# The second distance tile of each pair, made in the slot of the pair's first tile

## The chip, the cores and the metric

The kernel runs on one core of a Trainium2 chip. The metric is the device time of one execution in microseconds; lower is better. The engines have separate instruction queues and meet through semaphores: TensorE (PE in the profile, PEld for its weight loads), VectorE (DVE), ScalarE (ACT), GpSimd (POOL) and SyncE (SP), which here issues the DMAs.

## The reference

Two layers follow each other. The first is a chunked attention over `ctx` (32 batches, 128 channels, 1024 points; 8 heads, chunks of 64 points), with a residual and a normalisation along the points. The second works on the 30 nearest neighbours of each point, found by the distances between the columns of `ctx` of the same batch:

```python
def _knn(p, k):
    xx = jnp.sum(p * p, axis=1)
    pd = 2.0 * jnp.einsum('bdn,bdm->bnm', p, p) - xx[:, :, None] - xx[:, None, :]
    return jax.lax.top_k(pd, k)[1]
...
idx = _knn(x_loc, k)                       # x_loc is ctx, k is 30
pts = x_loc.transpose(0, 2, 1)
rel = pts[bidx, idx] - pts[:, :, None, :]  # first three channels are used
# rho, theta, phi of rel -> three small layers with batch norm -> softmax over the 30
agg = jnp.einsum('bnkc,bnk->bnc', xk, att)
return x + agg.transpose(0, 2, 1)
```

## The kernel before, in words

The kernel has three stages. `stage_a` does the attention, the distances, the search for the 30 nearest, and the gathering of their first three channels for all 32 batches; `stage_b` does the batch norms, `stage_e` the softmax and the weighted sum. Only `stage_a` is touched.

In `stage_a` the 1024 points of a batch are 8 tiles of 128 rows (`TILES`). Distances of tile t are a 128 x 1024 array, made as two halves of 512 columns (`distances(b, par, t, h)`; "D0" and "D1" in the prediction). Each half is two accumulated matmuls of TensorE (L407 and L409) into the one PSUM bank `pd_ps`, and a copy by ScalarE (its `distances`, through `move`, L588) into `pd_sb`, a ring of 4 tiles (`RING`). TensorE waits with a half until the copy before it is done (`pd_moved`), ScalarE waits with the first half of a tile until the tile that had its place has been sorted (`topk_done`).

VectorE works on tiles in pairs (0, 1), (2, 3), (4, 5), (6, 7). Four times (`RANKS`) it takes the 8 largest of each tile (MAX8, L866), finds their places (FIND_INDEX8, L871) and, the first three times, strikes them out (MATCH_REPLACE8, L873). The tiles of a pair alternate, so the second is wanted one MAX8 after the first. Between these it does the small steps of the attention: `largest(s)` (L896, the negated maximum of the scores, `mx`) behind the first and the third round, for the pair's first and second tile, each with `inverse` (L900, the reciprocal of the sums of exponentials of the tile before) ahead of it; `digits`, `row_stats` and `denoms` at fixed places. `gate` is a wait with a count.

TensorE and ScalarE go through the same slots t = 0 to 7, one for each tile, in an order written out by hand; h is the half of the batch and `quarter` the place in the half. A slot t has, in TensorE's order: turn_bits (quarter 0); unit; D0 of tile t + 2; unit; D1 of tile t + 2; unit; scores(t + 1); unit; turn_probs(t - 1); unit; values(t - 1); unit; the slot's extras; unit; unit. ScalarE has the copies that belong to them, and `exponents` (eight exponentials with their sums, L754) of tile t behind D0. The extras are: rows and project_values in slots 0 and 4, queries_keys in slots 2 and 6, squares in slot 3, norms in slot 5, and on ScalarE alone angles and rel_squares in slot 2 and roots in slot 4. Misc results use two PSUM banks in turn (`Misc`, `Moves`, `misc_ready`, `misc_moved`).

A unit is one rank of the 30 of the batch before: TensorE makes a one-hot matrix (`fill`, L482), ScalarE copies it (`one_hot`, `ohT`), TensorE multiplies it with the parts of the table (L503). TensorE is two fills ahead, ScalarE two copies. `unit_starts` gives 7, 8, 7 and 8 units to the slots of a half batch; each slot has eight calls of `unit()`, the last of which does nothing where there are 7.

scores(t + 1) wait for exponents(t) (`exp_ready`, one bank `s_ps`), `largest` waits for scores, exponents wait for `largest`. GpSimd normalises the exponentials (L1092, `normalise`) for turn_probs, spreads the keys (`spread_keys`, L1116, behind ScalarE's copy of `kt` in slots 2 and 6), multiplies and adds up what the units gathered, converts the digits (`convert`, L1126), and does the spherical coordinates of earlier batches (`sph_signs` and others), in an order of its own per slot.

A loop of the hardware runs over pairs of batches (`batches`: batches 0 to 3 and the last two are written out, the rest is `Fori`). In batch 0 there are no units.

Of the kernel before, what the change touches and what calls it, by code (L numbers as in the profile page):

```python
# [28 lines left out]
K = 30  # L29
EPS = 1e-5  # L30
TINY = 1e-20
TILES = T // P
QUADS = 2
QT = TILES // QUADS
# [111 lines left out]
def stage_a(nc, x, ctx, mask, w_in, b_in, w_out, b_out, consts, y_dram, cst, con, planes, idx_all, stats_all):  # L146
    OHR = 3
    XR = 97
    with ExitStack() as st:
# [121 lines left out]
        UNITS = QUADS * K  # L271
        NG = QUADS * GROUPS

        unit_starts = (0, 7, 15, 22, 30)
        slot_groups = [(4, 5), (0,), (1, 2), (3,)]

        FILLS = 31
# [26 lines left out]
        def there(d):  # L304

            return not isinstance(d, int) or d >= 0
# [54 lines left out]
        def _(pe):  # L361
# [37 lines left out]
            def distances(b, par, t, h):  # L399

                n = (b * TILES + t) * 2 + h

                if not (isinstance(n, int) and n < 1):
                    pe.wait_ge(pd_moved, n)
                if t == 0 and h == 0:
                    pe.wait_ge(xp_ready, b + 1)
                nc.tensor.matmul(pd_ps[:], ctx_s[:, par, bass.ts(t, P)], ctx_s[:, par, bass.ts(h, HALF)],  # L407
                                 start=True, stop=False)
                nc.tensor.matmul(pd_ps[:], ones3[0:XR, :], xp[0:XR, par, bass.ts(h, HALF)],  # L409
                                 start=False, stop=True).then_inc(pd_ready, 1)  # L410
# [74 lines left out]
            def gather(b, par, q, lo, hi, turned):  # L485

                if lo == 0:
                    pe.wait_ge(misc_moved, turned)
                    pe.wait_ge(split_step, (b + 1) * SPLITS)
                    fill(b, q, 0)  # L490
                    fill(b, q, 1)
                for k in range(lo, hi):
                    gu = b * UNITS + q * K + k
                    gi = q * GROUPS + k // GK
                    gg = b * NG + gi
                    if k + 2 < K:
                        fill(b, q, k + 2)
                    if k % GK == 0 and not (isinstance(gg, int) and gg < 2):
                        pe.wait_ge(g_moved, gg - 1)
                    pe.wait_ge(oh_moved, gu + 1)  # L500
                    for t in range(QT):
                        for part in range(PARTS):
                            m = nc.tensor.matmul(found_ps[gi % 2][:, k % GK, t, :], ohT[:, k % OHR, bass.ts(t, P)], tparts[:, par, part, :],  # L503
                                                 start=(part == 0), stop=(part == PARTS - 1))
                    if k % GK == GK - 1:
                        m.then_inc(g_ready, 1)

            def emit(b, j, par, first, last):
                misc = Misc(misc_base(b), first_bank(b, par))
                turned = None  # L510
                for t in range(TILES):
                    h, quarter = divmod(t, QT)
                    at = unit_starts[quarter]
                    end = unit_starts[quarter + 1]

                    def unit():
                        nonlocal at
                        if not first and at < end:
                            gather(b - 1, 1 - par, h, at, at + 1, turned)
                        at += 1  # L520

                    def ahead(half):

                        if t + 2 < TILES:
                            distances(b, par, t + 2, half)
                        elif not last:
                            distances(b + 1, 1 - par, t + 2 - TILES, half)

                    before = t > 0 or not first
                    nb, npar, nh = (b, par, 1) if h == 0 else (b + 1, 1 - par, 0)  # L530
                    ongoing = h == 0 or not last

                    if quarter == 0 and not first:
                        turned = turn_bits(misc, b - 1, h)
                    unit()
                    ahead(0)
                    unit()
                    ahead(1)
                    unit()
                    if quarter < QT - 1:  # L540
                        scores(b, par, t + 1)
                    elif ongoing:
                        scores(nb, npar, (t + 1) % TILES)
                    unit()
                    if before:
                        probs_in = turn_probs(misc, b if t > 0 else b - 1, (t - 1) % TILES)
                    unit()
                    if before:
                        moved = values(misc, (t - 1) % TILES, probs_in)
                    unit()  # L550
                    if quarter == 0 and before:
                        rows(misc, moved)
                    if quarter == 0:
                        project_values(misc, par, h)
                    if quarter == 2 and ongoing:
                        queries_keys(misc, npar, nh)
                    if t == 3 and not last:
                        squares(misc, b + 1)
                    if t == 5 and not last:
                        norms(misc, b + 1, 1 - par)  # L560
                    unit()
                    unit()

            def rows(misc, moved):

# [20 lines left out]
        def _(act):  # L586
# [38 lines left out]
            def distances(b, par, t, h, normed=None):  # L625
                s = b * TILES + t
                if t == 0 and h == 0:
                    act.wait_ge(misc_moved, normed)

                if h == 0 and not (isinstance(s, int) and s < RING):  # L630
                    act.wait_ge(topk_done, s - RING + 1)
                act.wait_ge(pd_ready, s * 2 + h + 1)
                move(pd_sb[:, t % RING, bass.ts(h, HALF)], pd_ps[:], scale=2.0,
                     bias=nxx[:, par, t:t + 1]).then_inc(pd_moved, 1)
# [36 lines left out]
            def emit(b, j, par, first, last):  # L671
                mv_ = Moves(misc_base(b), first_bank(b, par))
                normed = None
                for t in range(TILES):
                    h, quarter = divmod(t, QT)
                    at = unit_starts[quarter]
                    end = unit_starts[quarter + 1]

                    def unit():
                        nonlocal at  # L680
                        if not first and at < end:
                            gather(b - 1, h, at, at + 1)
                        at += 1

                    def ahead(half):
                        if t + 2 < TILES:
                            distances(b, par, t + 2, half)
                        elif not last:
                            distances(b + 1, 1 - par, t + 2 - TILES, half, normed)

                    before = t > 0 or not first
                    nb, nh = (b, 1) if h == 0 else (b + 1, 0)
                    ongoing = h == 0 or not last

                    if quarter == 0 and not first:
                        bits(mv_)
                    unit()
                    ahead(0)
                    exponents(b * TILES + t, t)
                    unit()  # L700
                    ahead(1)
                    unit()
                    unit()
                    if before:
                        turned_probs(mv_)
                    unit()
                    if before:
                        values(mv_, (t - 1) % TILES)
                    unit()
                    if quarter == 0 and before:  # L710
                        rows(mv_, b if t > 0 else b - 1, 0 if t > 0 else 1)
                    if quarter == 0:
                        project_values(mv_)
                    if quarter == 2 and ongoing:
                        queries_keys(mv_, nb, nh)
                    if t == 2:
                        if there(b - 3):
                            angles(b - 3)
                        if there(b - 2):
                            rel_squares(b - 2)  # L720
                    if t == 4 and there(b - 2):
                        roots(b - 2)
                    if t == 3 and not last:
                        squares(mv_, b + 1, 1 - par)
                    if t == 5 and not last:
                        normed = norms(mv_, 1 - par)
                    unit()
                    unit()

            def rel_squares(d):  # L730

# [44 lines left out]
            normed = norms(mv0, 0)  # L776
# [1244 lines left out]
```

## Time and profile before

| what | value |
|---|---|
| runs before | 5790.62 us median of 3 (5788.26 to 5792.64) |
| profiled execution, its own time | 5790.79 us |
| its span | 5788.7 us |
| mean granted clock of TensorE | 0.874 |
| busy: VectorE | 5127.8 us, 89% of the span |
| busy: TensorE | 4476.3 us, 77% |
| busy: ScalarE | 4035.6 us, 70% |
| busy: GpSimd | 3045.6 us, 53% |

The span is from the first to the last instruction; the execution's own time has 2.1 us more around it. `stage_a` ends at about 4025 us. Busy shares are over all three stages.

### The profile page before, as it was taken

The numbers are of one execution on the slowest core, as the hardware profiler recorded it, in microseconds if no ns is written. First come the engines' busy times: TensorE is split into PE (matmuls) and PEld (weight loads), VectorE is DVE, ScalarE is ACT, GpSimd is POOL, SyncE is SP. The second block draws the span as 40 slices with busy tenths as digits, with TensorE's granted clock in tenths as the row PEclk, the third lists the DMA queues.
The fourth block names the chain that finished last, engine by engine and source line by source line (L and its number), as shares of the span: only waits on it lengthen the run. The fifth ranks groups of instructions, "written<-read, shape, count | busy, mean of one in ns | idle before, by whom it ended". The sixth has DMA issues, their size and how long they took to land. (4 is left out here: it accounts for less than half of the span.)

```text
span 5788.7 us, 168877 instructions
## 1 busy us (share of the span) xinstructions
PE 4476.3 (77%) x62610; PEld 2718.6 (47%) x63182; DVE 5127.8 (89%) x7549; ACT 4035.6 (70%) x9505; POOL 3045.6 (53%) x3780
## 2 busy tenths in 40 slices
PE   5777777777777777777777777776395889999999
PEld 2444444444444444444444444443242666666666
DVE  7999989999989999998999998997398988888887
ACT  3777777777777777777777777776533766676666
POOL 3577777777777777777777777776400000000000
PEclk7888888888888898888888888887697899999999
DMA  0010000010000001000001000000000000000000
GB/s 29 16 31 16 16 17 16 17 31 16 17 16 17 17 16 32 16 17 16 17 17 31 17 16 17 16 16 12 1 0 8 25 30 27 30 26 30 26 30 26
DMA packets 135798, 114.60 MB, mean 20 GB/s; under 512 B 105344, under 2 KB 106112, under 8 KB 134784
## 3 DMA queue, kind: packets, MB, share of 16 engines
q1 hardware_dynamic: 134912, 102.73, 6.1%
q8 instruction: 563, 9.22, 0.7%
q14 instruction: 323, 2.65, 0.2%
HBM read 69.16 MB, written 33.55 MB: 18 GB/s over the span
## 5 line engine op out<-in xcount | busy, mean ns | idle before, releaser
L866 DVE MAX8 vals<-pd_sb 128x8 f32<-128x1024 f32 x1024 | 1200.6, 1211 | 302.2 <-ACT pd_sb L588 284.0
L588 ACT ACTIVATE ohT<-oh_ps 128x512 bf16<-128x512 f32 x1920 | 1152.0, 615 | 155.3 <-PE oh_ps L482 114.4
L871 DVE FIND_INDEX8 idx<-vals,pd_sb 128x8 uint16<-128x1024 f32 x1024 | 1244.6, 1218 | 0.0
L503 PEld LDWEIGHTS g_ps<-tparts,ohT 128*128 128x128 bf16 x23040 | 871.8, 99 | 380.9 <-issue 148.7
L503 PE MATMUL g_ps<-tparts,ohT 128*128 128x24 bf16 x23040 | 883.9, 175 | 81.6 <-issue 33.5
L873 DVE MATCH_REPLACE8 pd_sb<-vals,pd_sb 128x1024 f32<-128x1024 f32 x768 | 928.3, 1209 | 0.0
L1957 PEld LDWEIGHTS e_a_ps<-planes,e_oh 120*128 120x128 bf16 x24576 | 687.9, 97 | 299.5 <-issue 218.4
L482 PE MATMUL oh_ps<-bitsT,code 128*128 128x512 bf16 x1348 | 590.3, 442 | 293.4 <-ACT bitsT L772 155.7
L1727 ACT COPY e_at<-e_a_ps 128x512 f32<-128x512 f32 x512 | 543.1, 1061 | 356.1 <-PE e_a_ps L1957 349.8
L1957 PE MATMUL e_a_ps<-planes,e_oh 120*128 120x32 bf16 x24576 | 702.4, 178 | 83.2 <-DVE e_oh L1885 46.9
L754 ACT ACTIVATE sS<-s_ps,mx 128x64 f32<-128x64 f32 x2048 | 611.5, 329 | 169.4 <-DVE mx L896 168.1
L407 PE MATMUL pd_ps<-ctx_s 128*128 128x512 f32 x1024 | 656.3, 727 | 84.1 <-ACT pd_sb L588 82.9
L1885 DVE TENSOR_TENSOR e_oh<-e_pairs,e_iotan 120x2048 bf16<-120x2048 bf16 x512 | 623.9, 1219 | 3.4 <-PE e_a_ps L1957 1.1
L961 POOL TENSOR_TENSOR gsb<-gsb 128x240 f32<-128x240 f32 (+2 forms) x1152 | 544.5, 473 | 90.3
L482 PEld LDWEIGHTS oh_ps<-bitsT,code 128*128 128x128 bf16 x1920 | 192.8, 103 | 849.2 <-ACT ohT L588 360.8
L1116 POOL TENSOR_TENSOR kz<-kt,cst 128x1024 f32<-128x1024 f32 x256 | 484.3, 1902 | 172.2 <-ACT kt L588 101.0
L1971 PE MATMUL e_o_ps<-e_at,e_xT 128*128 128x512 f32 x1024 | 568.5, 650 | 0.2 <-ACT e_at L1727 0.2
L588 ACT ACTIVATE pd_sb<-pd_ps,nxx 128x512 f32<-128x512 f32 x512 | 366.2, 715 | 190.8 <-PE pd_ps L409 190.3
L1092 POOL TENSOR_TENSOR sS<-sS,rs 128x512 f32<-128x512 f32 x256 | 272.4, 1064 | 429.4 <-DVE rs L900 429.2
L754 ACT ACTIVATION_READ_ACCUMULATOR sS<-s_ps,mx 128x1 f32 x2048 | 455.1, 222 | 0.0
L958 POOL TENSOR_TENSOR gsb<-gsb,hi1h 128x480 f32<-128x480 f32 x384 | 439.9, 1146 | 12.5 <-DVE hi1h L835 8.7
L440 PE MATMUL s_ps<-xp,negs 32*64 32x512 bf16 x512 | 110.2, 427 | 370.2 <-ACT sS L754 367.0
(241 smaller groups left out, 7411.3 us busy)
## 6 DMA issues: line engine op xcount, KB each, us to landing
ctx_s<-in_ctx SPq DMA_DIRECT2D x32, 512.0 KB, 4.2
maskb<-in_mask_Bx1x_ff SPq DMA_DIRECT2D x32, 512.0 KB, 6.7
x_s<-in_x SPq DMA_DIRECT2D x32, 512.0 KB, 5.8
y_spill<-y_s SPq DMA_DIRECT2D x32, 512.0 KB, 3.0
e_y<-y_spill SPq DMA_DIRECT2D x32, 512.0 KB, 3.9
out<-e_o SPq DMA_DIRECT2D x64, 256.0 KB, 2.2
table<-in_ctx SPq DMA_DIRECT2D x96, 4.0 KB, 5.8
pd_sb<-in_shape_constants SPq DMA_DIRECT2D x1, 1180.0 KB, 5.4
```

Source lines behind the costliest of these rows:

```text
L407: nc.tensor.matmul(pd_ps[:], ctx_s[:, par, bass.ts(t, P)], ctx_s[:, par, bass.ts(h, HALF)], start=True, stop=False)
L482: nc.tensor.matmul(oh_ps[k % 2][:], code[:, k % KT, :], bitsT[:, k // KT, :], start=True, stop=True).then_inc(oh_ready, 1)
L503: m = nc.tensor.matmul(found_ps[gi % 2][:, k % GK, t, :], ohT[:, k % OHR, bass.ts(t, P)], tparts[:, par, part, :], start=(part == 0), stop ...
L588: return nc.scalar.activation(dst, src, func, scale=scale, bias=bias)
L754: m = nc.scalar.activation(sS[:, t % 2, hd, :], s_ps[:, hd, :], ACT.Exp, bias=mx[:, t % 2, hd:hd + 1], accum_out=rs[:, t % 2, hd:hd + 1])
L866: nc.vector.max(vals[:, i, :], pd_sb[:, (t + i) % RING, :]).then_inc(topk_step, 1)
L871: found = nc.vector.max_index(idx16[:, par, t + i, 8 * r:8 * r + 8], vals[:, i, :], work)
L873: nc.vector.match_replace(work, vals[:, i, :], work, REMOVED).then_inc(topk_step, 1)
L961: steps(nc.gpsimd.tensor_tensor(sums[:, :, 0:width], sums[:, :, 0:width], sums[:, :, width:2 * width], ALU.add))
L1885: v.tensor_tensor(oh[pp, g % RING], low.to_broadcast([QCOLS, NB // 2, LO, 2]), row.to_broadcast([QCOLS, NB // 2, LO, 2]), ALU.is_equal).th ...
L1957: m = nc.tensor.matmul(a_ps[g % 2][:, i].rearrange("p t e -> p (t e)"), oh[pp, g % RING, i // 2, :, i % 2], spr[q][pp, part, :, (g * NB + ...
L1971: m = nc.tensor.matmul(o_ps[q][:], xT[:, par, e, :], at[:, q, e].rearrange("p t n -> p (t n)"), start=(e == 0), stop=(e == HI - 1))
```

## The change

The distances of both tiles of the next pair are made in the even slot. Tile t + 2 stays where it was, in slot t with t even. Tile t + 3, which was made in slot t + 1 behind its first and its second unit, is made in slot t, behind `values` and one unit and ahead of the slot's extras. Odd slots make no distances. The calls of `unit()` become `units(place)` with a table of how many units stand at each of 8 places; between D0 and D1 of tile t + 3 (place 6) there is none, and the last place has one or two. The sums per slot are 7, 8, 7 and 8 as before. TensorE and ScalarE are changed alike.

```diff
-        unit_starts = (0, 7, 15, 22, 30)
+        units_at = ((1, 1, 1, 1, 1, 1, 0, 1),
+                    (1, 1, 1, 1, 1, 1, 0, 2),
+                    (1, 1, 1, 1, 1, 1, 0, 1),
+                    (1, 1, 1, 1, 1, 1, 0, 2))
+        unit_starts = [sum(sum(row) for row in units_at[:n]) for n in range(QT + 1)]
...
-                    def unit():
+                    def units(place):
                         nonlocal at
-                        if not first and at < end:
-                            gather(b - 1, 1 - par, h, at, at + 1, turned)
-                        at += 1
+                        n = units_at[quarter][place]
+                        if not first and n > 0:
+                            gather(b - 1, 1 - par, h, at, at + n, turned)
+                        at += n
...
-                    def ahead(half):
+                    def ahead(tiles, half):
-                        if t + 2 < TILES:
-                            distances(b, par, t + 2, half)
+                        if t + tiles < TILES:
+                            distances(b, par, t + tiles, half)
                         elif not last:
-                            distances(b + 1, 1 - par, t + 2 - TILES, half)
+                            distances(b + 1, 1 - par, t + tiles - TILES, half)
...
-                    unit()
-                    ahead(0)
-                    unit()
-                    ahead(1)
-                    unit()
+                    units(0)
+                    if t % 2 == 0:
+                        ahead(2, 0)
+                    units(1)
+                    if t % 2 == 0:
+                        ahead(2, 1)
+                    units(2)
...
-                    unit()
+                    units(5)
+                    if t % 2 == 0:
+                        ahead(3, 0)
+                    units(6)
+                    if t % 2 == 0:
+                        ahead(3, 1)
...
-                    unit()
-                    unit()
+                    units(7)
```

ScalarE's side has the same edit, with `exponents` where it stood, between `ahead(2, 0)` and `units(1)`.

## Rows read from the trace of the kernel before

**Rows 1.** The page's head: span and instructions.
```profile
span 5788.7 us, 168877 instructions
```

**Rows 2.** Waits from 365 to 4025 us: engine, line waited for, total, times, longest.
```profile
DVE vals L866 <- ACT pd_sb L588: 250.3, 31, 9.5
...
ACT sS L754 <- DVE mx L896: 139.7, 77, 5.2
```

**Rows 3.** Timeline of VectorE: start, duration, instruction, idle before it and releaser.
```profile
358.51 1.23 DVE L866 MAX8 vals<-pd_sb 128x8 f32<-128x1024 f32 x1 [5.51 <-ACT pd_sb L588]
...
2113.72 1.23 DVE L866 MAX8 vals<-pd_sb 128x8 f32<-128x1024 f32 x1 [8.36 <-ACT pd_sb L588]
...
2119.74 0.64 DVE L896 TENSOR_REDUCE mx<-s_ps 128x8 f32<-128x512 f32 x1
...
3994.10 1.23 DVE L866 MAX8 vals<-pd_sb 128x8 f32<-128x1024 f32 x1 [8.28 <-ACT pd_sb L588]
```

**Rows 4.** Timeline of TensorE, slots 4 and 5, and slot 4 a batch later.
```profile
2097.11 0.45 PE L503 MATMUL g_ps<-tparts,ohT 128*128 128x24 bf16 x12
2099.30 2.08 PE L568 MATMUL mi_ps<-oT,wT 128*128 128x512 f32 x2 [1.74 <-ACT oT L588]
...
2112.56 0.63 PE L440 MATMUL s_ps<-xp,negs 32*64 32x512 bf16 x2 [0.98 <-ACT sS L754]
2113.12 1.98 PE L444 MATMUL s_ps<-kz,qs 128*64 128x512 f32 x4
...
2219.84 1.09 PE L453 MATMUL mi_ps<-cst,sS 128*128 128x128 f32 x4 [2.58 <-POOL sS L1092]
...
2223.91 2.08 PE L568 MATMUL mi_ps<-oT,wT 128*128 128x512 f32 x2 [0.79 <-ACT oT L588]
```

**Rows 5.** Timeline of ScalarE, slots 4 and 5.
```profile
2101.50 0.69 ACT L588 ACTIVATE y_s<-mi_ps,bias 128x512 f32<-128x512 f32 x1 [1.76 <-PE mi_ps L568]
...
2108.02 0.69 ACT L588 ACTIVATE pd_sb<-pd_ps,nxx 128x512 f32<-128x512 f32 x1
...
2110.03 0.31 ACT L754 ACTIVATE sS<-s_ps,mx 128x64 f32<-128x64 f32 x1
...
2112.83 0.74 ACT L588 ACTIVATE pd_sb<-pd_ps,nxx 128x512 f32<-128x512 f32 x1
```

**Rows 6.** Timeline of TensorE: ends of slots 0, 2, 6, slot 4's start, slot 7.
```profile
2037.11 1.12 PE L568 MATMUL mi_ps<-oT,wT 128*128 128x512 f32 x2 [0.17 <-ACT oT L588]
...
2062.48 1.96 PE L416 MATMUL mi_ps<-ctx_s,wT 128*128 128x512 f32 x4
...
2086.26 2.05 PE L407 MATMUL pd_ps<-ctx_s 128*128 128x512 f32 x2
...
2130.66 1.12 PE L416 MATMUL mi_ps<-ctx_s,wT 128*128 128x512 f32 x2 [0.52 <-ACT oT L588]
...
2132.66 1.10 PE L407 MATMUL pd_ps<-ctx_s 128*128 128x512 f32 x2
2133.60 0.38 PE L409 MATMUL pd_ps<-xp,ones 97*128 97x512 bf16 x1
...
2134.76 1.13 PE L407 MATMUL pd_ps<-ctx_s 128*128 128x512 f32 x2 [0.27 <-ACT pd_sb L588]
2135.72 0.38 PE L409 MATMUL pd_ps<-xp,ones 97*128 97x512 bf16 x1
```

**Rows 7.** Timeline of ScalarE: copy of D0 in slots 1 and 7.
```profile
2042.47 0.69 ACT L588 ACTIVATE pd_sb<-pd_ps,nxx 128x512 f32<-128x512 f32 x1 [0.44 <-PE pd_ps L409]
...
2134.02 0.69 ACT L588 ACTIVATE pd_sb<-pd_ps,nxx 128x512 f32<-128x512 f32 x1 [0.53 <-PE pd_ps L409]
```

**Rows 8.** Timeline of GpSimd, slots 2 and 3 of two batches.
```profile
2070.91 1.35 POOL L1126 CAST bitsb<-bits 128x896 bf16<-128x896 uint16 x1 [0.82 <-DVE bits L827]
...
2193.72 1.04 POOL L1092 TENSOR_TENSOR sS<-sS,rs 128x512 f32<-128x512 f32 x1 [0.99 <-DVE rs L900]
...
2195.58 1.35 POOL L1126 CAST bitsb<-bits 128x896 bf16<-128x896 uint16 x1 [0.82 <-DVE bits L827]
```

More of the change, by code:

```diff
@@ L272, in stage_a @@
         NG = QUADS * GROUPS
-        unit_starts = (0, 7, 15, 22, 30)
+        units_at = ((1, 1, 1, 1, 1, 1, 0, 1),
[3 rows of a table added]
+        unit_starts = [sum(sum(row) for row in units_at[:n]) for n in range(QT + 1)]
+        assert unit_starts[QT] == K
         slot_groups = [(4, 5), (0,), (1, 2), (3,)]
@@ L513, in emit @@
                     at = unit_starts[quarter]
-                    end = unit_starts[quarter + 1]
-                    def unit():
+                    def units(place):
                         nonlocal at
-                        if not first and at < end:
-                            gather(b - 1, 1 - par, h, at, at + 1, turned)
-                        at += 1
-                    def ahead(half):
-                        if t + 2 < TILES:
-                            distances(b, par, t + 2, half)
+                        n = units_at[quarter][place]
[5 more added lines that the diff above has]
+                            distances(b, par, t + tiles, half)
                         elif not last:
-                            distances(b + 1, 1 - par, t + 2 - TILES, half)
+                            distances(b + 1, 1 - par, t + tiles - TILES, half)
                     before = t > 0 or not first
@@ L543, in emit @@
                         scores(nb, npar, (t + 1) % TILES)
-                    unit()
+                    units(3)
                     if before:
                         probs_in = turn_probs(misc, b if t > 0 else b - 1, (t - 1) % TILES)
-                    unit()
+                    units(4)
                     if before:
                         moved = values(misc, (t - 1) % TILES, probs_in)
-                    unit()
+                    units(5)
[4 more added lines that the diff above has]
+                        ahead(3, 1)
                     if quarter == 0 and before:
@@ L560, in emit @@
                         norms(misc, b + 1, 1 - par)
-                    unit()
-                    unit()
+                    units(7)
             def rows(misc, moved):
@@ L676, in emit, with units, ahead @@
                     at = unit_starts[quarter]
-                    end = unit_starts[quarter + 1]
-                    def unit():
+                    def units(place):
                         nonlocal at
[L681 to L687, printed above, removed]
+                        n = units_at[quarter][place]
+                        if not first and n > 0:
+                            gather(b - 1, h, at, at + n)
+                        at += n
+                    def ahead(tiles, half):
+                        if t + tiles < TILES:
+                            distances(b, par, t + tiles, half)
                         elif not last:
-                            distances(b + 1, 1 - par, t + 2 - TILES, half, normed)
+                            distances(b + 1, 1 - par, t + tiles - TILES, half, normed)
                     before = t > 0 or not first
@@ L696, in emit @@
                         bits(mv_)
-                    unit()
-                    ahead(0)
+                    units(0)
+                    if t % 2 == 0:
+                        ahead(2, 0)
                     exponents(b * TILES + t, t)
[L700 to L703, printed above, removed]
+                    units(1)
+                    if t % 2 == 0:
+                        ahead(2, 1)
+                    units(2)
+                    units(3)
                     if before:
                         turned_probs(mv_)
-                    unit()
+                    units(4)
                     if before:
                         values(mv_, (t - 1) % TILES)
-                    unit()
+                    units(5)
+                    if t % 2 == 0:
+                        ahead(3, 0)
+                    units(6)
+                    if t % 2 == 0:
+                        ahead(3, 1)
                     if quarter == 0 and before:
@@ L726, in emit @@
                         normed = norms(mv_, 1 - par)
-                    unit()
-                    unit()
+                    units(7)
             def rel_squares(d):
```

## The prediction

> **What bounds the kernel now.** Only the first stage, `stage_a`, is touched; it fills the first 4025 us or so of the span [rows 1], and almost all of it is 32 batches alike. I read the list of waits of this stretch first. VectorE, which sorts the distances, waits for one thing that is worth anything: `pd_sb` from ScalarE, 250.3 us in 31 waits [rows 2]. So it is not a little in every pair but one long wait in each batch. The timeline of VectorE says which: MAX8 of the pair's second tile waits 8.36 us at 2113.72, and the same wait stands 30 times from 358.51 to 3994.10 [rows 3]. Those 29 intervals give a period of (3994.10 - 358.51) / 29 = 125.4 us per batch. By the order in the code, the late tile is tile 7: its two halves D0 and D1 are made in slot 5, and the wait ends as ScalarE's copy of D1 lands (2112.83 plus 0.6) [rows 5].
>
> Second reading: why ScalarE is late there. It isn't loaded to the brim, but its slots and TensorE's are a chain of hand-overs, and I go by checkpoints, the first exponential of each slot ("exp(t)"). In the same stretch ScalarE waits for VectorE's maxima only 139.7 us [rows 2], that is 139.7 / (3660 / 125.4) = 4.8 us per batch. That number is the whole slack of the round that ScalarE and TensorE go through in a batch: without VectorE in their way they would need 125.4 - 4.8 = 120.6 us. VectorE without its wait would need 125.4 - 8.6 = 116.8 us; 8.6 is 250.3 / 29, for nearly all of that sum lies in the 29 long waits that fall into the stretch. So two things are near each other, and the slower of the two is not VectorE. What holds the period at 125.4 now is the loop from exp(2) through slots 2 to 4 and D1 of tile 7 to VectorE, and back over two and a half pairs of VectorE's work.
>
> **The change, part by part.** The counts of units per slot stay 7, 8, 7, 8, and since place 6 becomes 0 and the last place takes its unit, ahead of the extras and behind them there are as many units as before; this part costs nothing, and nothing needs to hide it, for the instructions are the same in the same order. No instruction is added or removed, no DMA moves, SP's and POOL's queues keep their order. What is left is that in each pair D0 and D1 of the second tile go from the odd slot (behind its first and second unit, D1 behind the exponentials) to the even slot, behind `values` and one unit, ahead of rows, project_values or queries_keys.
>
> What it removes: D1(7) would be wanted at about 2105.3. TensorE ends unit 5 of slot 4 at 2097.56 [rows 4]; a pair of halves takes 3.4 us (below), or 5 at the lower clock, so tile 7 is there by about 2103. The long wait for `pd_sb` goes, 8.6 us per batch at its face value.
>
> What it adds: the two halves share the one bank `pd_ps` and there is nothing between them now. Rows 6 show how such a couple runs: D0 2132.66 to 2133.98, copy, D1 2134.76 to 2136.10. That is 3.44 us of TensorE's queue, in which ScalarE does two copies of 0.57 to 0.69 us and otherwise waits. Whatever stands behind it in the slot is pushed by 3.44 us less the idle time that TensorE had there anyway:
> - Slot 0, rows: 0.17 idle [rows 6], push 3.3. Taken back: ScalarE no longer does D0 in slot 1, where it waited 0.44 and worked 0.69 [rows 7]. Net +2.1 at exp(1).
> - Slot 2, queries_keys: no idle [rows 6], push 3.4 on the copy of `kt`. POOL waits for that copy and then works without a stop through `sph_signs` to the normalising that slot 4's turn_probs waits for (2.58 us of TensorE waiting at 2219.84 in the next batch [rows 4]). In this chain POOL has idle time that swallows some of the push: 0.82 us in one batch, 0.99 + 0.82 in the next [rows 8]; mean 1.3. Net +2.1. ScalarE's own way into slot 3 (+3.4 less a D0 of 0.69) is the other branch, and it has that waiting as a cushion.
> - Slot 4, rows: idle 1.74 in one batch, 0.79 in the next [rows 4], push 1.7 or 2.65, mean 2.2, less D0 of slot 5 without a wait, 0.69 [rows 5]. Net +1.5 at exp(5).
> - Slot 6, queries_keys: the second projection waited 0.52 [rows 6]; push 2.9, less D0 of slot 7, 0.53 + 0.69 [rows 7]. Net +1.7.
>
> D1 taken out of the odd slots I count at nothing: it followed the exponentials, and there ScalarE's next dated step waits for TensorE's scores and turn_probs. If it were on the path in all four odd slots it would return 4 x 0.57 = 2.3 us; that is the bound on the good side. On the bad side is TensorE's clock. A pair of f32 matmuls takes 1.10 us at 2132.66 and 2.05 us at 2086.26 [rows 6], the first near the full level of 2.4 GHz, the second at 1.2 GHz. The odd slots lose a couple of matmuls just ahead of the exponentials, where TensorE idles, and the next scores may run at the lower clock, as 1.98 us at 2113.12 after 0.98 idle [rows 4]; I bound this by one such couple, +1.1, and one more in slot 4, +1.1. I take neither: slot 4 may as well gain, since its idle 1.74 us is filled.
>
> Sum: 2.1 + 2.1 + 1.5 + 1.7 = 7.4 us added to a round with 4.8 us of slack. New period 120.6 + 7.4 = 128.0, against 125.4: +2.6 us in each of 30 batches, +78 us. Against the profiled execution's own 5790.79 us (span 5788.7 [rows 1]), which is as good as the median 5790.62, that makes 5869 us.
>
> Rows 6 show a copy sitting between two halves of one bank, some 0.7 to 0.8 us from the end of D0 to the start of D1. The Trainium skill (Perfetto Trace Analysis, Optimizing Tensor Performance, Matmuls) says that independent matmul groups should go through different PSUM banks, so that emptying one overlaps the next group's matmuls. The trace agrees, and the change goes against it: before, a unit or the exponentials lay between the halves. As an estimate by that page and those rows: with a second bank for the distances the four insertions would cost 4 x 0.8 us less, 4.2 instead of 7.4, the period would be 120.6 + 4.2 = 124.8, and the time 5773 instead of 5869.
>
> Where the stall goes: VectorE runs the first ranks of pair (6, 7) at once and then stands at inverse(5), which needs exp(5) finished, and at largest(6), which needs scores(6) behind it.
>
> **Rivals.**
> 1. *The loop through largest(6) decides, and the kernel is a little faster.* In the trace exp(5) starts at 2110.03, scores(6) end at 2115.10, VectorE reads them only at 2119.74 [rows 3, 4, 5]. These 4.6 us are the most that a tile 7 in time can win. exp(5) itself comes 2.1 + 1.5 = 3.6 us later after exp(2). Gain 1.0 us per batch, 30 us: 5761. It holds if ScalarE's whole round does not bind, that is if the four slots add less than about 4.4 us. For it: D1's return of 2.3 us and a better clock would bring 7.4 near 4.4. Against: none of the pushes of slots 0, 2 and 6 rests on an unusual row.
> 2. *The long wait goes and nothing takes its place*: 30 x 8.6 = 258 us, 5533. It would need scores(6) to be there by 2111.4, before exp(5) even ends; only a round that became shorter by several us could do it.
> 3. *No difference*: the added time comes to 4.4 to 5.2 us, for instance 7.4 less the 2.3 of D1; 5.1 gives +9 us, 5800.
> 4. *Slower than forecast by the clock*: 7.4 + 2.2 = 9.6, +144 us, 5935. This is the far end of my forecast, not a case of its own.
>
> That the change doesn't do what it says is not a rival: both engines' queues are written by the same edit, and tile 7 is surely in time.
>
> **How the numbers follow.** Forecast (ScalarE's and TensorE's round binds) 0.70, with its own range 5815 to 5930; rival 1 0.17; rival 2 0.04; rival 3 0.09. 0.2%, 11.6 us, is about what a measurement of this kernel can tell from no change. Rivals 1 and 2 are the faster cases, 0.21; same 0.09; slower 0.70. The range leaves out rival 2 and the last piece of the clock's case, and takes in rivals 1 and 3: 5750 to 5920.
>
> **What the profile after would show.** MAX8's wait for `pd_sb`, 250.3 us now, falls to under 30. VectorE's RECIPROCAL L900 (inverse) and TENSOR_REDUCE L896 (largest) get waits on ScalarE's `sS` and TensorE's `s_ps` that they don't have now, 11 us per batch together, once per batch before largest(6) (about 8 us per batch under rival 1). ScalarE's wait for the maxima falls from 139.7 us to nearly nothing; if it stays above 80 the round isn't what binds, and the forecast is wrong at its root. ScalarE's wait for `pd_ps` rises by some 6 us per batch. The period of MAX8 of tile 7 goes to 128. What would make it wrong: pushes that the slots' ends swallow, so that exp(1), exp(5) and exp(7) come less than 1.5 us later in their round than now.

## The result and the profile after

The changed kernel takes 5815.73 us (median of 6, 5813.07 to 5832.56) against 5789.44 us for the kernel before (median of 6, 5786.63 to 5794.58). The ratio is 1.005, 95% interval 1.0037 to 1.0064: slower by 26 us. Of all the executions compared here and below one lies apart, 5776.13 us of slot4_denoms_late against 5658 to 5664 us for its five others, and the ratios leave it out. Forecast were 5869 us. The direction was right and the size three times too large. The profiled execution of the changed kernel has a span of 5823.6 us, 35 us above that of [rows 1].

The waits of the changed kernel from 365 to 4025 us, as in [rows 2]: engine, line waited for, total, times, longest.

```profile
ACT pd_sb L599 <- PE pd_ps L414: 336.7, 279, 2.5
...
DVE rs L917 <- ACT sS L771: 120.0, 38, 4.1
...
DVE mx L913 <- PE s_ps L449: 90.3, 47, 2.4
...
DVE rel L908 <- POOL rel L1032: 50.8, 29, 2.0
...
DVE vals L883 <- ACT pd_sb L599: 27.9, 21, 1.8
...
ACT vz L659 <- PE mi_ps L430: 22.7, 84, 0.3
```

And the last line of the same view for ScalarE alone, to 4050 us:

```profile
ACT sS L771 <- DVE mx L913: 2.2, 1, 2.2
```

VectorE's wait for `pd_sb` is down from 250.3 to 27.9 us. In its place stand 120.0 us at inverse, 90.3 us at largest, and 50.8 us at denoms (`rel`, L908), which the prediction didn't have. ScalarE's wait for VectorE's maxima, 139.7 us before, is as good as gone: the slack of its round is used up. ScalarE's wait for the distances in `pd_ps` has risen to 336.7 us. Before, in the same stretch, it was:

```profile
ACT pd_sb L588 <- PE pd_ps L409: 155.6, 149, 2.1
```

VectorE's timeline of one batch shows the three new waits' places and the digits:

```profile
2133.04 0.20 DVE L917 RECIPROCAL rs<-rs 128x8 f32<-128x8 f32 x1 [4.12 <-ACT sS L771]
...
2135.65 0.69 DVE L913 TENSOR_REDUCE mx<-s_ps 128x8 f32<-128x512 f32 x1 [2.40 <-PE s_ps L449]
...
2145.19 1.65 DVE L908 RECIPROCAL rel<-rel 128x240 f32<-128x240 f32 x1 [1.82 <-POOL rel L1032]
...
2154.40 0.61 DVE L844 TENSOR_TENSOR bits<-idx,bitval 128x896 uint16<-128x896 uint16 x1
2154.93 0.30 DVE L848 TENSOR_SCALAR hi<-idx 128x120 uint16<-128x120 uint16 x1
2155.26 0.66 DVE L852 TENSOR_TENSOR hi1h<-hi,hival 128x960 bf16<-128x960 uint16 x1
```

largest(6) now waits for the scores. In [rows 3] it found them ready.

**The round, slot by slot.** From ScalarE's timeline, for batches 4 to 29: the time from exp(t) to the moment at which ScalarE is ready for the next one (the start of the next less its wait for the maximum), in us.

| slot | before | after | difference | forecast |
|---|---|---|---|---|
| 0 | 13.04 | 14.62 | +1.6 | +2.1 |
| 1 | 10.48 | 11.58 | +1.1 | 0 |
| 2, 3, 4 together | 55.55 | 56.56 | +1.0 | +2.1 + 1.5 |
| 5 | 12.10 | 12.39 | +0.3 | 0 |
| 6 | 12.29 | 13.81 | +1.5 | +1.7 |
| 7 | 17.42 | 17.74 | +0.3 | 0 |
| round | 120.9 | 126.7 | +5.8 | +7.4 |
| wait for the maxima | 4.5 | 0.0 | | |

Singly, slot 2 is longer by 2.0 us (15.42 to 17.39), slot 3 by 0.9 (18.52 to 19.47), and slot 4 is shorter by 1.9 (21.59 to 19.70).

The period of the changed kernel is 126.7 us, all of it this round. Before it was 125.4. That is +1.3 us in 30 batches, 39 us, near the profiled execution's 35.

**Where slots 2 to 4 came out so well.** ScalarE's timeline of one batch after the change:

```profile
2074.21 0.31 ACT L771 ACTIVATE sS<-s_ps,mx 128x64 f32<-128x64 f32 x1
...
2086.01 0.69 ACT L599 ACTIVATE kt<-mi_ps,bias 128x512 f32<-128x512 f32 x1 [0.17 <-PE mi_ps L421]
...
2091.60 0.32 ACT L771 ACTIVATE sS<-s_ps,mx 128x64 f32<-128x64 f32 x1
...
2111.52 0.31 ACT L771 ACTIVATE sS<-s_ps,mx 128x64 f32<-128x64 f32 x1
...
2123.05 0.69 ACT L599 ACTIVATE y_s<-mi_ps,bias 128x512 f32<-128x512 f32 x1 [0.26 <-PE mi_ps L579]
...
2130.53 0.31 ACT L771 ACTIVATE sS<-s_ps,mx 128x64 f32<-128x64 f32 x1
```

The copy of `kt` ends 12.5 us after exp(2), against a mean of 9.95 before: pushed by 2.5 us, not 3.4. TensorE begins queries_keys there 9.89 us after exp(2) instead of 7.26, and the mean granted clock from exp(2) to that point is 1.00 instead of 0.88. In all_but_slot2 (below), where the clock is 1.00 as well and slot 2 has no second tile, it is 6.60 us: at one and the same clock the couple does push by 3.3 us. ScalarE copies `y_s` 7.5 us before exp(5); before the change it was 8.5 in this place (2101.50 to 2110.03, [rows 5]) and 9.0 in the mean. For `y_s` the reason is in TensorE's timeline. First the kernel before, project_values of slot 4 in two batches:

```profile
2101.31 2.49 PE L425 MATMUL mi_ps<-wT,ctx_s 128*64 128x128 f32 x32
...
2225.91 3.31 PE L425 MATMUL mi_ps<-wT,ctx_s 128*64 128x128 f32 x32
```

Then the changed kernel, slot 4: D0 and D1 of tile 7, the rows, project_values:

```profile
2118.62 1.11 PE L412 MATMUL pd_ps<-ctx_s 128*128 128x512 f32 x2
2119.56 0.38 PE L414 MATMUL pd_ps<-xp,ones 97*128 97x512 bf16 x1
2120.72 1.13 PE L412 MATMUL pd_ps<-ctx_s 128*128 128x512 f32 x2 [0.78 <-ACT pd_sb L599]
2121.68 0.38 PE L414 MATMUL pd_ps<-xp,ones 97*128 97x512 bf16 x1
2121.91 1.02 PE L579 MATMUL mi_ps<-oT,wT 128*128 128x512 f32 x2
2122.86 2.03 PE L430 MATMUL mi_ps<-wT,ctx_s 128*64 128x128 f32 x32
```

The couple takes 3.44 us, to the hundredth what [rows 6] gave. But the rows that follow take 1.02 us instead of 2.08 [rows 4], and project_values 2.03 instead of 2.49 and 3.31. From the start of the rows to the end of project_values slot 4 took 4.79 us in the mean before and takes 3.03 after (26 batches); slot 0, where nothing was slow before, went from 3.03 to 2.92. Before, TensorE had stood idle for 0.8 to 1.7 us just ahead of the rows, and in one batch for 2.58 us some 4 us ahead of them [rows 4]. The granted clock of these stretches (window, its length, busy time of TensorE and instructions, granted clock, DMA share and GB/s), first before and then after the change:

```profile
2099.30:2101.38 2.08, 2.08 (x4) 0.50 0.00 0
2101.31:2103.80 2.49, 2.48 (x33) 0.78 0.00 0
```

```profile
2121.91:2122.93 1.02, 1.02 (x5) 1.00 0.00 0
2122.86:2124.89 2.03, 2.03 (x34) 1.00 0.00 0
```

0.50 is 1.2 GHz and 1.00 is 2.4. Over the 26 batches the mean from the rows to the end of project_values is 0.64 before and 0.99 after. The distances fill the gap, and what stands behind them is done at the full clock.

**What the odd slots lost.** The scores of slots 1, 3, 5 and 7 follow the exponentials, where no distances stand any more. Their four matmuls took 1.12, 1.14, 1.56 and 1.44 us in the mean before and take 1.59, 1.98, 1.98 and 1.59 after; the granted clock in them went from 0.97, 0.95, 0.69 and 0.77 to 0.70, 0.50, 0.50 and 0.70. In slot 1 the changed kernel has both cases side by side: in 10 batches its scores take 1.08 us and the slot 10.68, in 13 batches 1.97 us and 12.31.

### The profile page after: what moved, and what is told of

Same layout as the page of the kernel before. It is cut to its first block and busy times, and to the rows that moved or that the text cites. A ratio compares the mean times of both kernels' runs of the same rounds, so it can differ in the third digit from the quotient of the medians.

```text
span 5823.6 us, 169449 instructions
## 1 busy us (share of the span) xinstructions
PE 4540.5 (78%) x63182; PEld 2676.2 (46%) x63182; DVE 5123.1 (88%) x7549; ACT 4049.7 (70%) x9505; POOL 3026.7 (52%) x3780
## 5 line engine op out<-in xcount | busy, mean ns | idle before, releaser
L599 ACT ACTIVATE ohT<-oh_ps 128x512 bf16<-128x512 f32 x1920 | 1128.4, 614 | 279.5 <-PE oh_ps L487 270.1
L883 DVE MAX8 vals<-pd_sb 128x8 f32<-128x1024 f32 x1024 | 1199.5, 1211 | 70.3 <-ACT pd_sb L599 54.9
L487 PE MATMUL oh_ps<-bitsT,code 128*128 128x512 bf16 x1920 | 833.7, 441 | 370.9 <-ACT ohT L599 214.9
L978 POOL TENSOR_TENSOR gsb<-gsb 128x240 f32<-128x240 f32 (+2 forms) x1152 | 544.7, 473 | 90.3
L771 ACT ACTIVATION_READ_ACCUMULATOR sS<-s_ps,mx 128x1 f32 x2048 | 467.3, 228 | 0.0
L445 PE MATMUL s_ps<-xp,negs 32*64 32x512 bf16 x512 | 123.6, 479 | 364.2 <-ACT sS L771 361.5
```

Source lines behind the costliest of these rows:

```text
L487: nc.tensor.matmul(oh_ps[k % 2][:], code[:, k % KT, :], bitsT[:, k // KT, :], start=True, stop=True).then_inc(oh_ready, 1)
L599: return nc.scalar.activation(dst, src, func, scale=scale, bias=bias)
L771: m = nc.scalar.activation(sS[:, t % 2, hd, :], s_ps[:, hd, :], ACT.Exp, bias=mx[:, t % 2, hd:hd + 1], accum_out=rs[:, t % 2, hd:hd + 1])
L883: nc.vector.max(vals[:, i, :], pd_sb[:, (t + i) % RING, :]).then_inc(topk_step, 1)
L978: steps(nc.gpsimd.tensor_tensor(sums[:, :, 0:width], sums[:, :, 0:width], sums[:, :, width:2 * width], ALU.add))
```

## The experiments

Each is compared with the kernel before on its own chip; ratios are to that. "Loop" is the way that sets VectorE's period, cut at events of the timelines, means over 25 batches, in us: from largest(2) to exp(2), to exp(5), to largest(6), and on VectorE back to the next largest(2) (that part is called VectorE's below); "digits" is the time of the three digit instructions of pair (6, 7), which lie in the last part.

```
kernel                largest2-exp2  exp2-exp5  exp5-largest6  largest6-largest2  period  digits
before                    0.7          55.6         9.7             59.5           125.5    2.6
changed                   4.8          56.6         5.1             60.3           126.8    1.5
only_slot4                0.7          56.0         5.1             62.9           124.7    4.4
all_but_slot4             1.2          57.2         9.7             61.3           129.4    4.5
all_but_slot2             4.4          54.9         5.1             60.1           124.5    1.5
first_half_only           0.7          54.3         9.7             61.2           126.0    4.2
unit_between              3.6          56.1         5.1             60.8           125.6    1.5
before_denoms_late        0.7          55.7         9.7             60.1           126.2    3.8
after_denoms_late         5.5          56.3         5.1             59.4           126.2    2.2
slot4_denoms_late         0.7          56.1         5.1             59.1           121.0    2.0
slot4_unit_between        0.7          55.5         5.1             59.3           120.5    2.2
load_after                5.2          56.4         5.1             60.7           127.4    1.5
load_before               0.7          55.4         9.7             59.7           125.5    2.7
```

A largest2-exp2 of 0.7 is VectorE's instruction itself: ScalarE stood ready. More than that is ScalarE behind, its round binding.

### Slot 4 alone, and all but slot 4

```diff
+        EARLY = (4,)                 # the other run: (0, 2, 6)
...
-                    if t % 2 == 0:
+                    if t % 2 == 0 or t - 1 not in EARLY:
                         ahead(2, 0)
...
-                    if t % 2 == 0:
+                    if t in EARLY:
                         ahead(3, 0)
```

and the same for the second halves, on both engines.

> Only tile 7 is made early (in slot 4); tiles 1, 3 and 5 are made in the odd slots as in the kernel before. Theory A (the pushes of the four slots lengthen the round of ScalarE and TensorE, 120.9 us before, 126.7 after, and that round binds after the change): slot 4's own push is small, the round stays near 121.2, tile 7 is in time and the loop through largest(6) wins 4 to 5 us per batch. Period about 121.2, 4.2 us x 30 = 126 us faster than before, 5664 us, ratio 0.978; ScalarE waits for the maxima less than 40 us in all. Theory B (the new wait at inverse(5) and largest(6) is the cost, whatever the other slots do): the kernel stays within 0.5% of the changed one, 5790 to 5820 us.

Measured: 5766.05 us against 5791.1, ratio 0.9954 (0.9941 to 0.9968). Theory B is out, for the wait at inverse(5) and largest(6) is there and the kernel is faster than before. ScalarE's slack is back, more of it than theory A's 40 us:

```profile
ACT sS L772 <- DVE mx L914: 103.1, 69, 3.0
DVE mx L914 <- PE s_ps L450: 69.7, 29, 2.4
DVE rs L918 <- ACT sS L772: 51.5, 29, 4.2
DVE rel L909 <- POOL rel L1033: 38.6, 25, 1.9
```

But it won 25 us, not 126. The table says where the rest went: exp5-largest6 gives the full 4.6 us, exp2-exp5 takes 0.4, and VectorE's own part takes 3.3 us. Of these 1.3 are the wait at denoms (38.6 us over 30 batches) and 1.8 the digits. Their rows in this run, VectorE and then GpSimd:

```profile
2126.65 1.10 DVE L845 TENSOR_TENSOR bits<-idx,bitval 128x896 uint16<-128x896 uint16 x1
2127.68 1.99 DVE L849 TENSOR_SCALAR hi<-idx 128x120 uint16<-128x120 uint16 x1
2129.70 1.32 DVE L853 TENSOR_TENSOR hi1h<-hi,hival 128x960 bf16<-128x960 uint16 x1
```

```profile
2125.37 4.14 POOL L1134 TENSOR_TENSOR kz<-kt,cst 128x1024 f32<-128x1024 f32 x2
2129.48 1.04 POOL L1110 TENSOR_TENSOR sS<-sS,rs 128x512 f32<-128x512 f32 x1
```

The same `hi` instruction takes 0.30 us in the changed kernel above, where GpSimd stands idle beside it, and 1.99 us here, from 2127.68 to 2129.67; GpSimd's spreading of the keys ends at 2129.51.

> Tiles 1, 3 and 5 are made early (slots 6, 0 and 2), tile 7 in slot 5 as before. Theory A: the round keeps nearly all that was added (5.8 us) and binds at about 126.3 to 127 us per batch: 5815 to 5840 us, ratio 1.004 to 1.009, and MAX8 of tile 7 waits again, 9 us or more per batch. Theory B (slot 4's couple is what costs): no slower than before, 5790 us.

Measured: 5911.49 us against 5791.1, ratio 1.0197 (1.0182 to 1.0212). The sign is theory A's, but the loss of 120 us is far above its 24 to 49. MAX8 waits as foreseen:

```profile
DVE vals L884 <- ACT pd_sb L600: 238.8, 29, 10.6
ACT sS L772 <- DVE mx L914: 58.9, 38, 3.5
```

ScalarE still waits for the maxima, so the round was not what bound this kernel; the loop through D1 of tile 7 did, with 3.9 us per batch more than before: 0.5 + 1.7 on ScalarE's side (the push of slot 2 lies in this loop) and 1.8 in VectorE's part, the digits again (4.5 instead of 2.6 us). 3.9 x 30 = 117 us. My reason for the number was wrong, and the digits belong into every such sum.

### Ten small copies more on ScalarE

```diff
+        spare = sb("spare", [P, 10, 8])
...
+                    if t == 6:
+                        for i in range(10):
+                            nc.scalar.activation(spare[:, i, :], wT[:, 0, 0:8], ACT.Identity)
```

> The changed kernel with ten small ScalarE copies (128x8, about 1.7 to 2 us together, results used nowhere) added at the end of slot 6's extras. Theory A (ScalarE's round has no slack left): the period grows by nearly their whole time, 1.5 to 2 us per batch, 45 to 60 us: 5861 to 5876 us. Theory B (VectorE's loop through largest(6) binds, ScalarE has slack ahead of slot 7): within 10 us of the changed kernel, 5816 us.

> The kernel before with the same ten copies in slot 6. There ScalarE waits 2.2 us for VectorE's maximum ahead of exp(7), so both theories expect them to be nearly hidden: 5790 to 5800 us. If the copies cost their full time here too, the comparison with the other run says nothing about slack.

Measured: in the changed kernel 5841.76 us, ratio 1.0086 (1.0072 to 1.01), 0.0036 above the changed kernel's 1.005, 21 us. In the kernel before 5790.58 against 5791.1, ratio 1.0 (0.9991 to 1.0009). The row of the copies in the first (instructions, shortest, median, longest in ns):

```profile
L748 ACT ACTIVATE spare<-wT x320: 192/196/240, 144.7 to 4057.3; 128x8 f32<-128x8 f32 x160
```

They overlap each other, and slot 6 is longer by 1.0 us, not by 1.7 to 2; the forecast of 45 to 60 us was too high by that. Of 1.0 us per batch, 30 us, 21 appear in the changed kernel and none before. In the kernel before the copies went into two waits of slot 6: that for the maximum fell from 2.2 to 1.7 us, and that for D0 of slot 7 from 0.53 us to nothing. So the same load costs nothing where ScalarE waits for VectorE (half of it would have been hidden in a wait for TensorE in any case), and most of its length where it doesn't.

### All but slot 2

The edit is as above, with `EARLY = (0, 4, 6)`.

> Tiles 1, 3 and 7 early (slots 6, 0, 4), tile 5 in slot 3 as before. By the sum of measured slots the round is 126.7 less about 2 to 3 us, 123.7 to 124.7, no longer above the loop through largest(6): 5750 to 5775 us, as with slot 4 alone, and ScalarE waits again for the maxima, but under 1 us per batch. If instead each early couple costs the same wherever it stands, it is a quarter better than the whole change: 5809 us less what slot 4 wins.

Measured: 5744.68 us against 5789.0, ratio 0.9922 (0.9909 to 0.9936). The time is 5 us below what was expected, but ScalarE waits for the maxima only 1.4 us in all, so the round still binds, at 124.3 us. Leaving slot 2 alone took 2.3 us off the round, more than the 1.0 that slots 2 to 4 had added together: slot 4 alone shortens its stretch.

### The two halves apart, and a unit between them

```diff
 first_half_only:
                     units(1)
-                    if t % 2 == 0:
-                        ahead(2, 1)
+                    ahead(2, 1)
...
                     units(6)
-                    if t % 2 == 0:
-                        ahead(3, 1)
 unit_between:
-        units_at = ((1, 1, 1, 1, 1, 1, 0, 1),
+        units_at = ((1, 1, 1, 1, 1, 1, 1, 0),
...
-                    (1, 1, 1, 1, 1, 1, 0, 1),
+                    (1, 1, 1, 1, 1, 1, 1, 0),
```

> Only D0 of tile t + 3 is made early; D1 stays in the odd slot behind the exponentials. The push of each slot is then one half, the round is near 122 and doesn't bind; but tile 7 again waits for exp(5): MAX8 waits 8 us or more per batch, and the loop through D1 gives 125.5 to 126 us, 5790 to 5805 us. If the early first half alone were enough, MAX8's wait would be gone.

Measured: 5815.21 us against 5789.0, ratio 1.0042 (1.0029 to 1.0056). The wait at MAX8 stays, 191.0 us, and exp5-largest6 is 9.7 as before: to come in time tile 7 needs D1, too, ahead of exp(5). ScalarE is not behind. Foreseen were 5790 to 5805 us; the digits take 4.2 us, 1.6 more than before, and the way from exp(2) to exp(5) is 1.3 shorter.

> The changed kernel with the unit of the last place put between D0 and D1 of tile t + 3 in all even slots (place 6 has 1, the last place 0). If the couple of halves in one bank costs because nothing is between them, 0.5 to 0.6 us of the extras' tail is hidden in it in each of four slots: the round falls from 126.7 to about 124.3 and the time by about 70 us to 5740 to 5765 us (ratio 0.992 to 0.996 of before). If the cost is only that the halves stand ahead of the extras, nothing changes: 5816 us.

Measured: 5791.72 us against 5789.0, ratio 1.0003 (0.9994 to 1.0012). The changed kernel's loss is gone. The time expected was 5740 to 5765 us. The round gave 1.2 us, half of what was expected: slots 0, 2 and 6 0.3 to 0.5 us each.

### denoms behind the digits

```diff
-                        if t == 6 and r == 1 and there(b - 2):
+                        if t == 6 and r == 3 and there(b - 2):
                             denoms(b - 2)
```

> Only tile 7 early, and VectorE's denoms two rounds of MAX8 later (behind the digits). In the run with only slot 4 VectorE waits 38.6 us for GpSimd at denoms, and the digits take 4.4 instead of 2.6 us per batch where GpSimd's spreading of the keys runs beside them. If the wait at denoms is the next cost, it goes: 1.3 us per batch, 39 us, 5727 us, plus or minus what the digits do, which now start 2.9 us earlier against GpSimd's work (1.6 us if nothing runs beside them, 4.4 us as they were): 5690 to 5770 us. If the round bound this kernel, nothing would change: 5766 us.

Measured: 5662.29 us against 5789.0, ratio 0.9778 (0.9764 to 0.9791). That is 28 us below the range expected, and nearly what theory A gave for slot 4 alone, 5664. The rows below are of the first stage, which in this profile ends 136 us before that of the kernel before (last exponential at 3883.1 against 4019.4 us) and has the period of slot4_unit_between within 0.5 us. Both costs of only_slot4 are gone: there is no wait at denoms, and the digits now meet short instructions of GpSimd:

```profile
2187.35 1.08 DVE L845 TENSOR_TENSOR bits<-idx,bitval 128x896 uint16<-128x896 uint16 x1
2188.35 0.52 DVE L849 TENSOR_SCALAR hi<-idx 128x120 uint16<-128x120 uint16 x1
2188.90 0.70 DVE L853 TENSOR_TENSOR hi1h<-hi,hival 128x960 bf16<-128x960 uint16 x1
```

> The kernel before with denoms behind the digits (the only edit). VectorE has no wait at denoms there, so nothing is won by that; only the digits start 1.6 us earlier against GpSimd's work and may take 1.5 to 4.4 us in place of 2.6. The loop through D1 of tile 7 carries that: between 32 us faster and 54 us slower, 5757 to 5843 us. If it were as fast as the run with slot 4 alone and denoms late (0.978), the early tile 7 would have nothing to do with that gain.

Measured: 5819.45 us against 5792.46, ratio 1.0047 (1.0034 to 1.006). Alone the edit loses 27 us, the digits grow to 3.8 us. Tile 7 in time alone wins 25 us, and the two together 127. So the gain of the run above is not this edit's; it is what tile 7 in time is worth once denoms and the digits don't take it back.

> The changed kernel with denoms behind the digits. The wait at denoms (50 us in all) goes. If ScalarE's and TensorE's round binds, that wait only becomes another wait of VectorE: 5810 to 5822 us, ratio 1.004 to 1.006 as before the edit. If VectorE's loop bound the changed kernel, 1.7 us per batch would come off, 50 us: 5766 us.

Measured: 5814.44 us against 5792.46, ratio 1.0033 (1.0021 to 1.0045). The 50.8 us at denoms are gone, the ratio is 0.0017 below the changed kernel's, 10 us, with intervals that overlap, and the waits at inverse and largest have grown from 120.0 and 90.3:

```profile
DVE rs L917 <- ACT sS L771: 135.1, 47, 4.1
DVE mx L913 <- PE s_ps L449: 114.3, 64, 2.4
```

VectorE does not bind the changed kernel.

### The best version

Slot 4 alone, denoms late, and a unit between D0 and D1:

```diff
-        units_at = ((1, 1, 1, 1, 1, 1, 0, 1),
+        units_at = ((1, 1, 1, 1, 1, 1, 1, 0),
...
+        EARLY = (4,)
...
-                        if t == 6 and r == 1 and there(b - 2):
+                        if t == 6 and r == 3 and there(b - 2):
```

> Only tile 7 early, denoms late, and in slots 0 and 4 the last unit ahead of the extras, in slot 4 between D0 and D1. The loop through exp(5) loses about 0.2 to 0.5 us of 121.0: 5645 to 5662 us, ratio 0.975 to 0.978; nothing if the unit's place is of no account.

Measured: 5650.67 us against 5792.46, ratio 0.975 (0.9737 to 0.9762), 142 us faster than before and 165 faster than the changed kernel. What is left of slack on both sides:

```profile
DVE mx L914 <- PE s_ps L450: 71.1, 30, 2.4
ACT sS L772 <- DVE mx L914: 40.8, 28, 2.1
DVE rs L918 <- ACT sS L772: 40.8, 28, 2.2
```

## Why the prediction was right or wrong

- *One wait per batch, at tile 7, and it goes.* Right: 250.3 to 27.9 us.
- *The stall goes to inverse(5) and largest(6).* Right in place. Forecast were 11 us per batch together; it is (120.0 + 90.3) / 29.2 = 7.2 (29.2 batches lie in the stretch), and 1.7 more at denoms, which waits for GpSimd's `sph_denoms` now that VectorE comes earlier to it. That wait had been overlooked. after_denoms_late shows that it costs the changed kernel little, some 10 us of its 50 by the ratios; only_slot4 and slot4_denoms_late show that it would cost a faster one.
- *The round of ScalarE and TensorE binds.* Right and shown: no wait for the maxima, the small copies cost time only there, and leaving out denoms' 50 us of waiting gives back some 10. ScalarE's wait for `pd_ps` rose by (336.7 - 155.6) / 29.2 = 6.2 us per batch, and 6 were forecast.
- *The slack is 4.8 us.* 4.5 in the mean of the slots.
- *The couple costs 3.44 us.* Right to the hundredth. unit_between shows that part of it can be hidden with one bank still. No run has a second bank, so the estimate of 5773 us for that stays open. At the lower clock the couple's matmuls, 1.32 + 1.34, would be 5.3 us and the couple 6.1, not the 5 of the prediction; tile 7 would still have been there by 2103.7, ahead of 2105.3.
- *The sum of the pushes, 7.4 us.* This is the step that failed: it measures 5.8. Slots 0 and 6 were near (3.8 forecast, 3.1 measured). The terms of slots 2 and 4, 2.1 + 1.5, measure 1.0 together, and the runs part them. The couple of slot 4 lengthens the way from exp(2) to exp(5) by 0.4 us alone (55.6 to 56.0, only_slot4) and shortens it by 0.6 behind the three others (57.2 to 56.6); forecast were +1.5. That of slot 2 costs 1.6 (54.9 to 56.6); forecast were 2.1. The sentence "I take neither: slot 4 may as well gain, since its idle 1.74 us is filled" had named the mechanism and priced it at nothing: rows and project_values of slot 4 became 1.76 us shorter with the clock. They take 3.01 us in only_slot4 too, but 4.35 in all_but_slot4, so it is slot 4's own couple that does it. The idle time ahead of the rows was well read, 1.2 us in the mean of 26 batches against 1.27 from the two of [rows 4]. On the other side slots 1, 5 and 7, counted at nothing, took 1.7 us together, 1.1 of it slot 1. That is the prediction's "bad side", a lower clock for the scores once the distances ahead of them are gone, and the batches of slot 1 bear it out: in half of them the scores are slow and the slot is 1.6 us longer. That compares batches of one run and is no experiment. In slots 5 and 7 the scores are slower as well, but how much that adds to these slots is not shown.
- *The sign of being wrong.* exp(1) came 1.6 us later, exp(7) 1.5, but exp(5) only 1.0 after exp(2), less than the 1.5 that the prediction asked for.
- *From 5.8 to the time.* 120.9 + 5.8 = 126.7 against 125.4 is 39 us by the profile and 26 us by the medians. (The profiled execution of the changed kernel was 10 us above its median.) With a slack of 4.5 a term of 1.6 us too much in 7.4 more than doubles the result: the excess over a slack is a small difference of two large numbers.
- *Rival 1, "a little faster, 5761".* It didn't hold for the change. With slot 4 alone the round stops binding, and the kernel took 5766. Its price was right for a wrong reason, for exp(5) was pushed by 0.4 and not by 3.6 us, and denoms and digits took what that left. That 5766 is near 5761 is luck. Its condition was also too wide: a gain of 1.0 us per batch needs a round under 124.4, so less than 3.8 us added and not 4.4.
- *Rivals 2 and 3.* The long wait went and others took its place, and the added time was above the 5.2 us up to which the kernel would have stayed as it was. unit_between, with 4.5 us added to the round, is there: 1.0003.

The digits were in no sum. In the changed kernel they happened to lie well (1.5 instead of 2.6 us). In four of the runs they took 1.2 to 1.9 us more than before and upset the expectation.

## What to carry to other kernels

Before moving work to where it is wanted, find which round binds next, and how much slack it has. Here one of four tiles was late, moving four used the slack up, and moving that one, with two small repairs, gave 2.5%. Price together with a push the clock of what stands behind it: here 3.4 us of matmuls put into idle time gave 1.8 us back in one slot, and those taken away cost up to 1.6 us in a batch of another. And where two numbers nearly cancel, give the difference the width of both.

## What the hardware did that was not expected

The VectorE instruction `hi` on 128x120 uint16 takes 0.28 to 0.31 us wherever no GpSimd instruction overlaps it, 453 times in the thirteen traces. Beside GpSimd it took up to 2.02 us: 1.99 in only_slot4, where it started inside the second of the two instructions that spread the keys, and 1.13 in before_denoms_late, where it started at 2272.91 inside the normalising and GpSimd's next instruction came at 2273.84. The two others of the digits took 0.61 and 0.66 us alone, 1.10 and 1.32 us beside GpSimd. The Trainium skill (SBUF — State Buffer, Who interferes with whom) says that VectorE and GpSimd share a port pair as an exclusive lock: an instruction of VectorE in a 2-port mode and one of GpSimd block each other for the whole of the one that was issued first, and one of VectorE with two inputs in SBUF contends with one of GpSimd that reads SBUF. These rows agree: `hi` ended 0.16 us behind the spreading instruction inside which it had started, and GpSimd's own couple took 4.14 us instead of 3.76 beside the digits. That `hi` runs in a 2-port mode is inferred, no row shows the mode. Whether the digits start 1.5 us before the spreading (2154.40 and 2155.92 in the changed kernel) or 1.3 us after its start (2126.65 and 2125.37 in only_slot4) makes 1.5 or 4.4 us of them. The largest excess over the kernel before, 1.9 us, is by an estimate 30 x 1.9 = 57 us, 1% of the kernel.
